# Four fused layers on one Trainium2 core: the last layer's first attention pass starts seven groups later, and expert tiles are stored before the next load

## What is computed

```python
xn = _layernorm(x)
x = x + _L3_attn_ref(xn, ...) + _L3_ffn_ref(xn, ...)

def _L3_attn_ref(x, W_qkv, b_qkv, W_out, b_out):      # 16 heads of width 8
    qkv = (x @ W_qkv + b_qkv).reshape(b, s, h, 3 * hd)
    logits = einsum('bshd,bkhd->bhsk', q, k) / sqrt(hd)
    logits = where(k_pos > q_pos, -inf, logits)       # causal
    attn = softmax(logits)
    return einsum('bhsk,bkhd->bshd', attn, v).reshape(b, s, d) @ W_out + b_out

def _L3_ffn_ref(x, router_w, w1, b1, w2, b2):         # 8 experts, top 2
    probs = softmax(x_flat @ router_w.T)
    top_k_probs, top_k_idx = top_k(probs, 2)          # then normalized to sum 1
    for e in range(8):
        h = new_gelu(x_flat @ w1[e].T + b1[e])
        output = output + cw[:, e:e + 1] * (h @ w2[e].T + b2[e])
```

## Time and profile before

| what | value |
|---|---|
| median of 3 runs | 2345.53 us (2345.46 to 2348.88) |
| span of the profiled execution | 2297.3 us |
| median less that span | 48.2 us |
| PE, DVE, ACT, POOL busy over the span | 82%, 80%, 63%, 56% |
| layer 3 in the profile | 1507 to 2297.3 us |
| slot 0 begins | 1556 us |
| slots 3, 7, 12, 13 begin | 1654.1, 1851.0, 2080.3, 2125.7 us |
| slots 14, 15, 16 begin | 2171.0, 2203.1, 2234.3 us |

### The profile page before, as it was taken

How to read it: one execution, slowest core, us unless ns; L and a number is a source line. 1 busy time by engine, 2 the same in 40 slices (tenths; PEclk the granted TensorE clock), 3 DMA queues, 4 the chain that set the end, 5 groups by cost and what they waited for, 6 DMA issues and landing times. The chain is left out here.

```text
span 2297.3 us, 33048 instructions
## 1 busy us (share of the span) xinstructions
PE 1874.2 (82%) x10244; PEld 991.1 (43%) x10244; DVE 1827.5 (80%) x2453; ACT 1443.0 (63%) x2641; POOL 1292.7 (56%) x938
## 2 busy tenths in 40 slices
PE   6797879787978797787987599975688888889886
PEld 5233333333333333233563488852244444445432
DVE  6499999999999999987868899968665665666683
ACT  2576767676767676556344777741467656766666
POOL 5498989898989898932225255554611111111265
PEclk9899989998999898898989799965799999999998
DMA  3254544454444454540011000012332233233212
GB/s 76 86 160 137 157 142 158 139 156 147 158 144 151 146 149 147 154 127 16 14 48 43 1 0 0 0 45 72 102 109 75 87 112 96 72 90 97 64 35 75
DMA packets 156264, 217.56 MB, mean 95 GB/s; under 512 B 31706, under 2 KB 68586, under 8 KB 155498
## 3 DMA queue, kind: packets, MB, share of 16 engines
q1 hardware_dynamic: 152026, 207.41, 29.6%
q0 software_dynamic: 4096, 8.40, 1.4%
HBM read 196.59 MB, written 23.86 MB: 96 GB/s over the span
## 5 line engine op out<-in xcount | busy, mean ns | idle before, releaser
L717 PE MATMUL ps<-m_hC,ident 128*128 128x512 f32 x1024 | 511.7, 644 | 132.1 <-DVE m_hC L1005 132.1
L914 POOL TENSOR_TENSOR m_dBx<-m_du,m_rowB 128x1024 f32<-128x1024 f32 x256 | 603.7, 2387 | 7.3 <-DMA m_rowB<-bc_rows 7.0
L3087 DVE TENSOR_REDUCE a_mx<-ps 128x2 f32<-128x1024 f32 (+2 forms) x320 | 350.8, 1117 | 139.5 <-PE ps L2649 102.5
L2877 ACT ACTIVATE a_pT<-ps 128x512 f32<-128x512 f32 (+2 forms) x640 | 318.6, 558 | 222.5 <-PE ps L2672 196.5
L840 ACT ACTIVATE ps<-m_delta,m_A 128x512 f32<-128x512 f32 x512 | 339.7, 685 | 119.5 <-DVE m_h L996 118.6
L717 PEld LDWEIGHTS ps<-m_hC,ident 128*128 128x128 f32 x1024 | 202.5, 205 | 424.8 <-issue 232.7
L996 DVE TENSOR_TENSOR_SCAN m_h<-ps,m_carry,m_dBx 128x512 f32<-128x512 f32 x256 | 311.2, 1266 | 9.0 <-ACT ps L840 9.0
L996 DVE TENSOR_TENSOR_SCAN m_h<-ps,m_dBx 128x512 f32<-128x512 f32 x256 | 295.9, 1206 | 19.1 <-ACT ps L840 18.5
L3248 POOL TENSOR_SCALAR_AFFINE_SELECT a_pT<-a_pT 128x512 f32<-128x512 f32 x104 | 66.1, 635 | 427.3 <-ACT a_pT L2877 427.0
L924 POOL TENSOR_TENSOR m_hC<-m_h,m_rowC 128x1024 f32<-128x1024 f32 x80 | 194.3, 2429 | 69.3 <-DVE m_h L996 69.0
L1005 DVE TENSOR_TENSOR m_hC<-m_h,ps 128x1024 f32<-128x1024 f32 x176 | 214.9, 1221 | 21.2 <-ACT ps L850 7.1
(11 more groups left out here) (400 smaller groups left out, 3427.8 us busy)
## 6 DMA issues: line engine op xcount, KB each, us to landing
m_rowB<-bc_rows SPq DMA_DIRECT2D x256, 256.0 KB, 4.4
m_rowC<-bc_rows SPq DMA_DIRECT2D x256, 256.0 KB, 4.2
a_w<-in_L3f_w1T SPq DMA_DIRECT2D x39, 256.0 KB, 2.9
a_w<-in_L3f_w2T SPq DMA_DIRECT2D x39, 256.0 KB, 3.8
expert_rows<-in_zero_rows SPq DMA_DIRECT2D x39, 128.0 KB, 2.6
a_xs<-expert_rows SPq DMA_DIRECT2D x39, 128.0 KB, 2.9
expert_out<-a_y SPq DMA_DIRECT2D x39, 128.0 KB, 3.7
qk_parts<-a_part SPq DMA_DIRECT2D x18, 256.0 KB
```

The source lines that it names most:

```text
L717: mm = pe.matmul(ps[:, bankY + c, :], k.ident[:], hC[:, n % NBUF, c, :], start=False, stop=n % NS == NS - 1)
L914: pool.tensor_tensor(dBx[:, n % NBUF], du[:, i % 2, :, chunk(i, x)], rowB[:, n % 4, :].unsqueeze(1).to_broadcast([P, HALF, CH]), ALU.mult) ...
L2877: act.activation(dst, src, ACT.Exp).then_inc(t_read, 1)
L3087: dve.tensor_reduce(mx[:, c % 2, :, es[0]:es[0] + len(es), t, x // CH], src, AX_X, ALU.max)\
```

## The change

`DELAY = 7` moves every item's first pass seven groups later: `front(s, g)` gives the item and units for a group, so groups 0 to 6 of slot `s` hold the last twelve units of item `s - 1`, and groups 7 to 11 the first eight of item `s`. Slots are as many as before; slot 0's first seven groups are empty, and slot 16 gets twelve units. The final reduction of the maxima opens group 7, `turn_max` and `turned_max` close it, and `split_max` stands in group 8 of POOL's loop, in the same slot whose groups 0 to 6 ended the first pass. On SP the tiles' store goes ahead of the load, and a slot's first two tiles go ahead of `maxima`. The scatters are spread anew over slots 0 to 2 (25, 32 and 7 instead of 23, 24 and 17). The count of the routing (`count`, `slots`) stays behind the first two units. `last_two` moves seven groups later.

```diff
+DELAY = 7
-SPREAD = ((0, 0, 0, 1, 1, 1, 1, 1, 1, 1, 1, 1, 1, 1, 2, 2, 2, 2, 2, 2), (1, 1, 1, 1, 1, 1, 1, 1, 1, 1, 1, 1, 1, 1, 1, 1, 2, 2, 2, 2))
-SCATTER = (1, 1, 2, 2, 2, 2, 2, 2, 2, 1, 0, 0)
+SPREAD = ((0, 0, 0, 1, 1, 1, 1, 1, 1, 1, 1, 1, 2, 2, 2, 2, 2, 2, 2, 2), (1, 1, 1, 1, 1, 1, 1, 1, 2, 2, 2, 2, 2, 2, 2, 2, 2, 2, 2, 2))
+SCATTER = (1, 1, 1, 1, 1, 1, 1, 0, 0, 0, 0, 0)
+def front(s, g):
+    c, part = divmod(s * GROUPS + g - DELAY, GROUPS)
+    return c, range(sum(SHARE[:part]), sum(SHARE[:part + 1])) if 0 <= c < NI else ()
+
+def largest_known(s, g):
+    return s - 1 if g == DELAY and 0 <= s - 1 < NI else None
...
-        last_two = t_at["E", NI - 2, 0, 0]
+        last_two = t_at["E", NI - 2, DELAY, 0]
...
                 for s in range(SLOTS):
+                    for kt in tiles_of(s)[:2]:
+                        store_tile(kt)
+                        if kt + 4 < NTILE:
+                            load_tile(kt + 4)
                     if 0 <= s - 1 < NI:
                         maxima(s - 1)
                     if s == FIRST_SLOT - 1:
                         for kt in range(4):
                             load_tile(kt)
-                    for kt in tiles_of(s):
+                    for kt in tiles_of(s)[2:]:
+                        store_tile(kt)
                         if kt + 4 < NTILE:
                             load_tile(kt + 4)
-                        store_tile(kt)
...
-                    if 0 <= s - 1 < NI:
-                        turn_max(s - 1)
                     for g in range(GROUPS):
-                        units = range(sum(SHARE[:g]), sum(SHARE[:g + 1])) if front else ()
+                        f, units = front(s, g)
...
+                        if largest_known(s, g) is not None:
+                            turn_max(largest_known(s, g))
...
                 for s in range(SLOTS):
-                    if 0 <= s - 1 < NI:
-                        split_max(s - 1)
+                    if s == 1:
+                        split_max(0)
...
                     if s >= 2:
-                        pool.wait_ge(parts, min(s, NI))
+                        pool.wait_ge(parts, min(s - 1, NI))
                         for g in range(GROUPS):
+                            if g == DELAY + 1 and s - 1 < NI:
+                                split_max(s - 1)
```

More of the change, by code:

```diff
@@ L2319, in ring_tables @@
         back = 0 <= b < NI
-        if 0 <= s - 1 < NI:
-            add(s_at, ("Z", s - 1))
         for g in range(GROUPS):
@@ L2325, in ring_tables @@
                     add(t_at, ("E", b, g, i))
-            units = range(sum(SHARE[:g]), sum(SHARE[:g + 1])) if s < NI else ()
+            f, units = front(s, g)
             for i in units[:1]:
-                add(s_at, ("S", s, i))
+                add(s_at, ("S", f, i))
             for j, kt in enumerate(tiles_of(s)):
@@ L2332, in ring_tables @@
             for i in units[1:]:
-                add(s_at, ("S", s, i))
-            if s == 0 and g == 0:
+                add(s_at, ("S", f, i))
+            if s == 0 and g == DELAY:
                 add(s_at, ("C",))
@@ L2352, in ring_tables @@
                 add(s_at, ("Y", bb, u))
+            if largest_known(s, g) is not None:
+                add(s_at, ("Z", largest_known(s, g)))
     return s_at, t_at
@@ L2785, in _ @@
                 for s in range(SLOTS + 1):
-                    f, b = s, s - 2
-                    front, back = f < NI, 0 <= b < NI
-                    if 0 <= s - 1 < NI:
-                        turn_max(s - 1)
+                    b = s - 2
+                    back = 0 <= b < NI
                     for g in range(GROUPS):
-                        units = range(sum(SHARE[:g]), sum(SHARE[:g + 1])) if front else ()
+                        f, units = front(s, g)
                         if back:
@@ L2795, in _ @@
                             score(f, i)
-                        if back and not front and len(TU[g]) > 2:
+                        if back and not units and len(TU[g]) > 2:
                             scoreT(b, g, 2)
@@ L2801, in _ @@
                             sums(b - 1, GROUPS - 1)
-                        if back and front and len(TU[g]) > 2:
+                        if back and units and len(TU[g]) > 2:
                             scoreT(b, g, 2)
@@ L3167, in _ @@
                 for s in range(SLOTS + 1):
-                    first, b = s, s - 2
-                    if 0 <= s - 1 < NI:
-                        turned_max(s - 1)
+                    b = s - 2
                     for g in range(GROUPS):
-                        units = range(sum(SHARE[:g]), sum(SHARE[:g + 1])) if first < NI else ()
+                        c = largest_known(s, g)
+                        if c is not None:
+                            dve.wait_ge(s_read, s_at["S", c, len(SU) - 1] + 1)
+                            if c >= 2:
+                                dve.wait_ge(s_done, s_at["Z", c - 2] + 1)
+                            dve.tensor_reduce(m[:, c % 2, :], mx[:, c % 2].rearrange("p r e t x -> p (r e t) x"),
+                                              AX_X, ALU.max).then_inc(max_done, 1)
+                        first, units = front(s, g)
                         for i in units[:1]:
@@ L3199, in _ @@
                             residual(x, u)
-                    if first < NI:
-                        dve.wait_ge(s_read, s_at["S", first, len(SU) - 1] + 1)
-                        if first >= 2:
-                            dve.wait_ge(s_done, s_at["Z", first - 2] + 1)
-                        dve.tensor_reduce(m[:, first % 2, :], mx[:, first % 2].rearrange("p r e t x -> p (r e t) x"),
-                                          AX_X, ALU.max).then_inc(max_done, 1)
+                        if c is not None:
+                            turned_max(c)
                     for n in GATHER.get(s - 1, ()):
```

## The result

| | us (median) | against the kernel before |
|---|---|---|
| before, measured beside it | 2347.2 (2345.5 to 2356.4, 4 runs) | |
| after | 2378.45 (2376.1 to 2384.4, 4 runs) | 1.014 (1.0121 to 1.0159) |
| forecast | 2369.0, range 2347 to 2387, from 2345.5 | 1.010 |

A forecast was written before the change was run, and what follows sets the result against it. PE was taken to bound slots with experts, POOL's scatter chain the stretch between slots 2 and 3. Terms 2.2 - 14.9 + 20.8 + 8.1 + 4.3 + 3 = +23.5 us gave 2369.0 us, range 2347 to 2387.

The forecast's parts named there:

- The sign: Whole kernel: the change makes it slower, chance 0.78.
- late maxima: Starts of slots after 3 to 12: PE's first scoreT waits for six DMAs issued behind two tiles, +20.8 us.
- start of the layer: Ahead of slot 3: scatters, a split and six DMAs still hold tile 0's load, so PE turns it +2.2 us later.
- turning hidden: Slot starts behind tile 0: 13 waits of 1.14 us for the turning of the maxima go, -14.9 us.
- stores first: SP's queue: stores ahead of loads free the output buffers sooner, but DVE is not the bound; costed at nothing.
- the delay itself: Groups 0 to 3: DVE's extra score units are taken up at no cost, or cost up to 0.5 us a slot.
- PE's clock behind them: Behind six new waits of 3 to 5 us: a third of 6 x 1.5 us, +3 us, between 0 and 9.
- slots 14 to 17: Layer's end: the split behind POOL's gathers makes PE wait, +8.1 us; twelve units more in slot 16, +4.3 us.
- the step on the lead-in: Ahead of slot 3: twelve units leave, worth 13 us, but PE only idles from about 1641 until tile 0.
- more of the same: Rival, chance 0.18: the clock falls after each wait and the third tile's load comes late, +37.5, 2383 us.
- The 48 us outside the span: Whole kernel: the median's 48.2 us above the profiled span, added unchanged to the new span.

The follow-up runs named there:

- run 4: The changed kernel with the six DMAs of the maxima sent behind a slot's first tile instead of its second: 2322.8 us, 1.0098 of the kernel before.
- run 3: The kernel before with only the turning of the maxima moved behind the next slot's second group, no first pass delayed: 2296.6 us, 0.9971.
- run 1: The kernel before, unchanged, measured again with a new profile: 2301.1 us beside 2302.6, 0.9994.
- run 2: The kernel before with only each tile's store put ahead of the next load: 2299.05 us, 0.9988 of the kernel before.
- run 5: The changed kernel, unchanged, measured again with a new profile: 2356.5 us, 1.0221 of the kernel before.
- run 10: The kernel of run 9 with the list of shares turned round, so each group has as many score units as before: 2339.8 us, 0.9969.
- Run 8: The kernel of run 3 with a delay of three groups and the maxima sent ahead of a slot's tiles: 2309.5 us, 1.0022 of the kernel before.
- run 11: The kernel before with stores ahead of loads and the turning moved behind the second group in slots 4 to 14 only: 2337.8 us, 0.9969.
- run 9: The kernel of run 4 with the split ahead of group 7's gathers from slot 14, and DVE's additions gated on item 15's split: 2348.85 us, 1.0008.
- runs 9 to 12: run 9, run 10, run 11, and the kernel before with stores first and the turning moved in slots 4 to 13 only: 2337.4 us, 0.9968.

## Why the prediction was right, and where it was not

The sign held and the time lay in the range, the second in part by luck: measured again beside a before of 2303.3 the same kernel costs 53 us, more than the 41.5 that the top of the range allows. The largest cost forecast, the late maxima, was there, and about as large as forecast; three other terms were far too small. By traces, from runs 1 to 5 (the differences add up to the whole by construction; run 4 less run 3 holds several edits at once, and rows of a few us are no larger than what two profiles of the same code differ by):

| term | forecast | measured |
|---|---|---|
| start of the layer | +2.2 | +5.0 (0.8 of it in layers 0 to 2) |
| turning hidden | -14.9 (13 waits, slots 4 to 16) | -11.2 (run 3 less run 1, 11 waits, slots 4 to 14) |
| stores first | 0 | -3.8 (run 2 less run 1) |
| the delay itself | 0 | +9.6 (run 4 less run 3, 5.8, and the 3.8 that run 4's stores gain) |
| late maxima: waits | +20.8 | +17.0 (eight waits) |
| PE's clock behind them | +3 | +18.1 (run 5 less run 4, less 17.0; some 12 by the means) |
| slots 14 to 17 | +12.4 | +21.9 |
| tail | 0 | -0.5 |
| sum | +23.5 | +56.1 of span |

*Start.* The scatters ended at 1655.6, as said. SP's first load came at 1662.55 (forecast 1661.9) and tile 0 at 1668.67 (1667.7); PE and SP of the changed kernel:

```profile
1662.55 0.40 SPq L2556 DMA_DIRECT2D a_xs<-expert_rows  x1
```
```profile
1662.63 0.61 PE L2691 MATMUL ps<-a_q,a_k 51*128 51x512 bf16 x2 [18.60 <-DMA a_q<-a_m_parts]
1668.67 0.66 PE L2734 MATMUL ps<-ident,a_xs 128*128 128x128 f32 x2 [3.71 <-DMA a_w<-in_L3f_w2T]
```

PE stood idle from 1644 on, as the step on the lead-in had it: the twelve units that left it bought nothing. The term is 5.0 and not 2.2 because before's new profile had the load at 1658.10, 1.7 us earlier than the earlier trace rows, and tile 0 came 1.0 us later than forecast. The split that left the chain of scatters was to save 2.0 us; from first start to last the chain takes 84.0 us against 84.7, since a pause of 1.25 us for a score unit now stands in it.

*The turning.* I took the mean of all 16 waits, 1.14 us, for the 13 that count. In the same profile those 13 sum to 13.6 us, not 14.9: the two longest, of 1.78 us, stand ahead of slot 3.

*The maxima.* The path was built right. Slot 11 again, SP's and DVE's rows of the changed kernel:

```profile
2100.79 0.42 DVE L3140 TENSOR_TENSOR a_y<-ps,a_b 128x256 f32<-128x256 f32 x1 [1.02 <-PE ps L2754]
```
```profile
2101.25 0.39 SPq L2568 DMA_DIRECT2D expert_out<-a_y  x1
2102.27 0.38 SPq L2556 DMA_DIRECT2D a_xs<-expert_rows  x1
2104.78 3.72 SPq L2545 DMA_DIRECT2D a_q<-a_m_parts  x6
```
```profile
a_q<-a_m_parts SPq DMA_DIRECT2D x6, 4.0 KB, 2.0
```

From DVE's end at 2101.21 to `scoreT` at 2109.71 are 8.5 us, forecast 9.5: the issues start at 2104.78, 3.57 behind that end (forecast 3.8), and these DMAs land 2.0 us after issue, not the 2.6 taken from the earlier trace rows. The Trainium skill's fixed cost of about 2.0 us, which it gives for a DMA issued by GpSimd ("DMA: Bandwidth & Descriptors", section "Anatomy of one DMA") and which I had set aside, is also what this trace has for these six, which SP issues; by it this term would have been some 5 us smaller, 16 against the 17.0 measured.

*PE's clock, the step that failed most.* I priced a fall at one down-projection that ran slow, 1.5 us, and let a third of six waits pay it. The slow stretch behind a wait is not one instruction long: at slot 12's start it lasts for the eight us shown above, the clock fell behind seven of the eight waits and not a third of them, and the 18.1 us over eight waits are 2.3 us each, as much as the wait itself (2.1 in the mean; by the means of several profiles 1.5). The Trainium skill, "TensorE: Matmul & The Clock Gate", section "Why this matters for your kernels", warns that the clock falls back in idle gaps between bursts of matmuls; this trace agrees. The 9 us that I had for a fall behind every long wait were half of what came. The rival "more of the same" named this mechanism, with half its price, and stood at 0.18; its other half did not come, since PE waits for no tile's load between slots 3 and 14.

*The delay itself.* I held two units in groups 2 and 3 for free or up to 0.5 us a slot. Putting the old shares back gave 9.1 us of time (run 10), so most of the delay's cost lies in the shares that it moved and not in the delay itself; how they cost it is open. Run 8 loses 13.0 us with a shift of three, which moves the shares in another way, so it fits but does not single them out. *Stores first* was costed at nothing and gained 3.5 us (run 2).

*The end.* This term was 9.5 us too small. The twelve units and the late split are there, but the waits of 1.6 and 1.7 us for the maxima at the starts of slots 15 and 16 did not come; slot 17's wait is 8.1 us and not 4.8, and slot 16 begins with one of 3.3 us for DVE that no step had:

```profile
2281.68 0.39 PE L2663 MATMUL ps<-a_k,a_q 48*128 48x512 bf16 x2 [3.30 <-DVE a_mx L3106]
2314.24 0.61 PE L2691 MATMUL ps<-a_q,a_k 51*128 51x512 bf16 x2 [8.10 <-DMA a_q<-a_m_parts]
```

PE's clock is in this term too: 0.90 over the stretch against 1.00 before (the windows of the result). The wait for DVE, and some 3 of slot 17's 8.1 us, come from `combine`: at the end of slot 15 it stands ahead of slot 16's first score units, which had not been there before, and in slot 16 its 16 additions shut POOL out between the last gathers of group 7 and the split. POOL's and DVE's rows of the changed kernel:

```profile
2301.31 4.19 POOL L3273 DMA_INDIRECT a_h<-expert_out,l_slot  x1 [0.30 <-ACT a_pT L2896]
...
2306.77 0.30 POOL L3258 CAST a_m_parts<-a_mT 32x128 bf16<-32x128 f32 x1
```
```profile
2300.41 4.27 DVE L3170 SCALAR_TENSOR_TENSOR x_tm<-l_xn,l_cwr,x_tm 128x128 f32<-128x128 f32 x16
```

*The 48 us outside the span* of before, which I carried over as a constant, were no such thing: a profiled run's span lies 2 us below its own time (2299.2 and 2301.07 for before, 2374.2 and 2376.08 for the changed kernel's first profile). It did no harm, since it was added to both sides. Why the change costs 53 us beside a before of 2303.3 and 31 beside one of 2347.2 stays open. Of the 18.9 us by which the changed kernel's two profiles differ, 17.4 lie before slot 3's group 2.

## What to carry to other kernels

When work is moved later, follow each small transfer behind it through the issuing queue: here the compute was well hidden, and six 4 KB DMAs behind two tiles' loads instead of one cost 34 us. Price a wait of TensorE by the wait and the slow stretch behind it, read from a place in the trace where it already happens, and not by the first slow instruction alone. And before giving an idea up, take out its side effects one at a time: with the maxima sent behind the first tile, the additions gated and the shares turned round, the same seven groups' delay ends at 0.9969 of the kernel before, where the plainer edit, the turning moved behind group 1 with the stores first, ends too (run 11, beside the same before). Last, ask of a gain or loss of a few us in one stretch of one profile whether two profiles of the same code agree better than that.

## What was not expected of the hardware

- POOL can stand still while DVE runs `scalar_tensor_tensor` on two SBUF inputs: a cast of 0.28 us took 8.02 beside 8.47 us of additions, a gather's issue of 0.95 us took 4.19 and 6.52, each ending within 0.9 us of DVE's last addition. The Trainium skill, "SBUF — State Buffer", section "Who interferes with whom", says that a DVE instruction with two SBUF inputs contends with a GpSimd instruction that reads SBUF; these rows agree, and in run 9 an order in which the split does not fall into the additions gave it its usual time back. It is not the rule for every instruction, though: in before's new profile two gathers pass at 1.03 and 1.00 us beside such additions, and only the third is held:

```profile
2252.09 1.03 POOL L3253 DMA_INDIRECT a_h<-expert_out,l_slot  x1 [0.30 <-ACT a_pT L2877]
2253.42 1.00 POOL L3253 DMA_INDIRECT a_h<-expert_out,l_slot  x1 [0.30 <-issue]
2254.73 2.06 POOL L3253 DMA_INDIRECT a_h<-expert_out,l_slot  x1 [0.31 <-ACT a_pT L2877]
```
```profile
2251.68 4.28 DVE L3151 SCALAR_TENSOR_TENSOR x_tm<-l_xn,l_cwr,x_tm 128x128 f32<-128x128 f32 x16
```

- Behind seven of eight waits of 1 to 3 us in a busy stretch PE's clock fell, at slot 12's start to half rate for at least eight us; with the waits gone the mean granted clock from slot 3 to slot 14 was 1.00 in run 4 and 0.98 in run 9.
- In the first profile of the changed kernel and in those of runs 9 to 12 ACT stood idle (in run 11 with its scores ready) 7 to 10 times and 22.9 to 37.0 us in all, and the profile names nothing of this core for it ("remote"); in the other nine profiles it never did. It happens in slots 0 to 3 and from slot 14 on, in the main where POOL scatters and gathers; the 64 scatters take 96 to 109 us from first start to last in these five profiles, 83 to 86 in the others. That is most of the some 42 us between before's two times, but before has no profile with such a time, so for it this is not shown. ACT's timeline of run 11, slot 16 behind its group 6:

```profile
2268.59 2.06 ACT L2882 ACTIVATE a_pT<-ps 128x512 f32<-128x512 f32 x4 [2.43 <-remote]
2275.76 4.03 ACT L2882 ACTIVATE a_pT<-ps 128x512 f32<-128x512 f32 x8 [5.11 <-remote]
```

What holds it was not found.
